# Attention softmax: the negated row maximum as the bias of ScalarE's exponential, VectorE as the copier of the transposed probabilities, other step distances

## The reference

```python
qkv = x @ Wqkv_w.T + Wqkv_b
q = qkv[..., :nf].reshape(nb, ns, 12, 16).transpose(0, 2, 1, 3)
k = q
v = q
w = jnp.einsum('bhqd,bhkd->bhqk', q, k) * (1.0 / jnp.sqrt(16.0))
mask = jnp.tril(jnp.ones((ns, ns)))
w = jax.nn.softmax(w * mask - 1e10 * (1.0 - mask), axis=-1)
a = jnp.einsum('bhqk,bhkd->bhqd', w, v)
return a.transpose(0, 2, 1, 3).reshape(nb, ns, nf) @ Wproj_w.T + Wproj_b
```

## Time and profile before

| | |
|---|---|
| median of three runs | 4598.12 us (4597.52 to 4603.08) |
| the profiled execution's own time | 4601.28 us |
| its span, first to last instruction | 4599.5 us |
| mean granted TensorE clock | 0.949 |
| busy over the span: TensorE, VectorE, ScalarE, GpSimd | 90%, 71%, 52%, 70% |

### The profile page before, as it was taken

How to read it: one execution, slowest core, us unless ns; L and a number is a source line. 1 busy time by engine, 2 the same in 40 slices (tenths; PEclk the granted TensorE clock), 3 DMA queues, 4 the chain that set the end, 5 groups by cost and what they waited for, 6 DMA issues and landing times. The chain is left out here.

```text
span 4599.5 us, 63372 instructions
## 1 busy us (share of the span) xinstructions
PE 4145.6 (90%) x17184; PEld 2234.8 (49%) x17184; DVE 3250.3 (71%) x5016; ACT 2413.6 (52%) x4880; POOL 3215.3 (70%) x1671
## 2 busy tenths in 40 slices
PE   7988958996999999999999999999999974999994
PEld 5666646672344344344334434433433434666773
DVE  5777762121899999999899999999989986112124
ACT  3566632223766766666676666667667544222221
POOL 3233213441999999999999999999999971444441
PEclk7999987997999999999999999999999987999997
DMA  1000023451343333433333333333333321344466
GB/s 34 25 21 23 15 64 87 122 151 52 108 119 116 120 112 112 124 112 120 120 115 112 112 115 121 113 115 116 122 112 115 111 85 49 109 117 118 134 185 227
DMA packets 264754, 478.66 MB, mean 104 GB/s; under 512 B 37044, under 2 KB 174084, under 8 KB 264548
## 3 DMA queue, kind: packets, MB, share of 16 engines
q1 hardware_dynamic: 235776, 403.02, 27.8%
q0 software_dynamic: 28032, 73.17, 6.4%
q10 hardware_dynamic: 740, 0.49, 0.0%
HBM read 409.60 MB, written 41.81 MB: 98 GB/s over the span
## 5 line engine op out<-in xcount | busy, mean ns | idle before, releaser
L1818 POOL TENSOR_TENSOR m_xh<-m_u,m_Bb 128x1536 f32<-128x1536 f32 x512 | 1776.9, 3539 | 58.1 <-DVE m_u L1689 44.9
L1745 PE MATMUL bank<-m_xh,ident 128*128 128x512 f32 x3072 | 1459.7, 611 | 36.3 <-POOL m_xh L1807 36.3
L1787 DVE TENSOR_TENSOR_SCAN bank<-bank,m_xh 128x512 f32<-128x512 f32 x864 | 1039.0, 1216 | 45.1 <-ACT bank L1774 41.9
L1774 ACT ACTIVATE bank<-m_dt,m_Ac 128x508 f32<-128x508 f32 x1536 | 1024.7, 683 | 38.4 <-DVE m_xh L1787 38.4
L1745 PEld LDWEIGHTS bank<-m_xh,ident 128*128 128x128 f32 x3072 | 577.2, 194 | 828.6 <-issue 737.1
L1787 DVE TENSOR_TENSOR_SCAN m_xh<-bank,m_xh 128x512 f32<-128x512 f32 x672 | 787.7, 1207 | 71.5 <-ACT bank L1774 66.0
L1807 POOL TENSOR_TENSOR m_xh<-m_xh,m_Cb 128x1536 f32<-128x1536 f32 x224 | 791.2, 3532 | 4.8 <-DVE m_xh L1787 4.5
L1798 DVE TENSOR_TENSOR m_xh<-bank,m_Cb 128x512 f32<-128x512 f32 x864 | 580.8, 672 | 9.8 <-DMA m_Cb<-BC_rows 9.8
L1204 ACT ACTIVATE f1t_h<-bank,f1t_b 128x512 f32<-128x512 f32 (+1 forms) x276 | 142.8, 589 | 471.3 <-PE bank L1239 471.3
L1593 PE MATMUL bank<-m_xp,m_dg 128*128 128x512 f32 x768 | 352.4, 601 | 3.7 <-DVE m_u L1689 1.4
L1134 POOL DMA_INDIRECT rows_y<-f1t_y,f1t_home x142 | 140.3, 988 | 272.7 <-DVE f1t_y L1175 243.4
(11 more groups left out here) (367 smaller groups left out, 6002.0 us busy)
## 6 DMA issues: line engine op xcount, KB each, us to landing
m_Bb<-BC_rows SPq DMA_DIRECT2D x256, 512.0 KB, 4.9
m_Cb<-BC_rows SPq DMA_DIRECT2D x256, 512.0 KB, 4.1
f1t_w<-f_w SPq DMA_DIRECT2D x46, 576.0 KB
m_r<-m_dt POOLq DMA_DIRECT2D x32, 768.0 KB, 7.4
f1t_w1a<-f_w SPq DMA_DIRECT2D x46, 384.0 KB
f0t_w<-f_w SPq DMA_DIRECT2D x22, 576.0 KB
f1c_yg<-rows_y SPq DMA_DIRECT2D x16, 768.0 KB, 8.3
f1t_w1b<-f_w SPq DMA_DIRECT2D x92, 96.0 KB
```

The lines of the kernel that those rows point to most:

```text
L1745: mm = pe.matmul(bank[:, c, :], K.ident[:, :], xh[n % NX][:, c, :], start=False, stop=(d == 1 and n == NS - 1))
L1774: act.activation(o[:, :, lo:hi], seqs(dt[d][:, c, :])[:, :, lo:hi], ACT.Exp, scale=Ac[:, c, n:n + 1]).then_inc(s_dA, 1)
L1787: dve.tensor_tensor_scan(o, bank[:, RING[d][p], way], xh[n % NX][:, c, way], 0.0, ALU.mult, ALU.add).then_inc(s_h, 1)
L1818: pool.tensor_tensor(xh[n % NX][:, :, :], u[d][:, :, :], Bb[q % RB][:, n % QN, :].unsqueeze(1).to_broadcast([P, DC, TOK]), ALU.mult).then_ ...
```

## The change

VectorE takes the maximum with its sign turned (`negate=True`) and no longer subtracts. ScalarE takes the exponential straight from the score bank, head by head, since the bias is one value a row: three instructions of 128 columns in place of one of 384, each adding one to `s_exp`. The scale 1/4 moves into Q: the copies into qT multiply by 16^(-1/4), which the product of Q with itself squares; the mask's constant shrinks by the same factor 4. The copy of the transposed probabilities moves from ScalarE (`act_pT`) to VectorE (`dve_pT`, right behind `dve_unit`). A score bank is now free when the three exponentials are done. Q's last block is waited for only before the last of the three heads. All distances are new.

```diff
@@ -180,7 +180,7 @@
         s_xn, s_gam, s_h1, s_h1kept = sem("xn_ready"), sem("gamma_done"), sem("h1_ready"), sem("h1_kept")
         s_z, s_zTps, s_zT = sem("z_ready"), sem("zTps_ready"), sem("zT_ready")
         s_qps, s_q = sem("qps_ready"), sem("q_ready")
-        s_sc, s_mx, s_sub, s_exp = sem("scores_ready"), sem("max_ready"), sem("sub_ready"), sem("exp_ready")
+        s_sc, s_mx, s_exp = sem("scores_ready"), sem("max_ready"), sem("exp_ready")
         s_pT, s_pTc, s_pv = sem("probsT_ready"), sem("probsT_copied"), sem("pv_ready")
         s_OT, s_O, s_V = sem("heads_copied"), sem("heads_back"), sem("V_cleared")
         s_ri, s_at, s_aT, s_aTc = sem("rowsum_inv"), sem("att_ready"), sem("attT_ready"), sem("attT_copied")
@@ -188,11 +188,11 @@
 
         OB, TB, FB = (5, 6), 4, 7
         UN = G * RG
-        LE, LT, LU, LV = 3, 4, 5, 9
-        LC, LO, LN, LA, LB, LR, LH = 9, 10, 12, 14, 14, 15, 15
-        PE_AT = {"emb0": 2, "emb1": 3, "zT0": 10, "zT1": 11, "q0": 11, "q1": 12, "q2": 13, "q3": 14, "q4": 15}
+        LE, LT, LU, LV = 0, 2, 2, 7
+        LC, LO, LN, LA, LB, LR, LH = 7, 8, 9, 10, 11, 13, 14
+        PE_AT = {"emb0": 2, "emb1": 3, "zT0": 9, "zT1": 10, "q0": 11, "q1": 12, "q2": 13, "q3": 14, "q4": 15}
         DVE_AT = {"onehots": 0, "emb0": 2, "emb1": 3, "stats1": 3, "norm1": 4, "stats2": 7, "norm2": 8}
-        ACT_AT = {"keep": 10, "zT0": 10, "zT1": 11, "q0": 12, "q1": 12, "q2": 13, "q3": 14, "q4": 15}
+        ACT_AT = {"keep": 8, "zT0": 9, "zT1": 10, "q0": 11, "q1": 12, "q2": 13, "q3": 14, "q4": 15}
 
         WEIGHTS = (
             (gam[:, :], A["ln_gamma"].partition_broadcast(P)), (bet[:, :], A["ln_beta"].partition_broadcast(P)),
@@ -219,7 +219,7 @@
                 pool.iota(col_i[:, :], pattern=[[0, 2]], base=0, channel_multiplier=1).then_inc(cleared, 1)
                 pool.wait_ge(cleared, 2)
                 pool.affine_select(out=mask[:, :, :], in_=mask[:, :, :], compare_op=ALU.is_ge,
-                                   fill=-4.0 * BIG, base=0, pattern=[[0, HC], [-1, P]], channel_multiplier=1).then_inc(cleared, 1)
+                                   fill=-BIG, base=0, pattern=[[0, HC], [-1, P]], channel_multiplier=1).then_inc(cleared, 1)
                 pool.wait_ge(cleared, 3)
                 pool.iota(col_i[64:128, 1:2], pattern=[[0, 1]], base=0, channel_multiplier=1).then_inc(cleared, 1)
                 pool.wait_ge(cleared, 4)
@@ -360,12 +360,13 @@
                 dve.wait_ge(s_sc, n + 1)
                 s_ps = bank[:, u % RG, 0:HC * P].rearrange("p (c k) -> p c k", c=HC)
                 if u >= NE or not isinstance(g, int) or g > 0:
-                    dve.wait_ge(s_pT, n - NE + 1)
-                dve.reduce_max(mx[:, u % NE, :], s_ps, AX).then_inc(s_mx, 1)
-                dve.wait_ge(s_mx, n + 1)
-                dve.tensor_tensor(S[:, u % NE, :, :], s_ps,
-                                  mx[:, u % NE, :].unsqueeze(2).to_broadcast([P, HC, P]),
-                                  ALU.subtract).then_inc(s_sub, 1)
+                    dve.wait_ge(s_exp, (n - NE + 1) * HC)
+                dve.reduce_max(mx[:, u % NE, :], s_ps, AX, negate=True).then_inc(s_mx, 1)
+
+            def dve_pT(dve, g, u):
+                n = g * UN + u
+                dve.wait_ge(s_pT, n + 1)
+                dve.tensor_copy(ST[:, u % NE, :, :], bank[:, TB, 0:HC * P].rearrange("p (c k) -> p c k", c=HC)).then_inc(s_pTc, 1)
 
             def dve_norm_att(dve, g, j):
 
@@ -393,6 +394,7 @@
                 for u in units:
                     if u < UN:
                         dve_unit(dve, g, u)
+                    unit(dve_pT, dve, g, u, LU)
                     for step, lag in ((dve_residual, LH), (dve_norm_att, LN)):
                         tile(step, dve, g, u, lag)
                     for name, step in front.items():
@@ -427,7 +429,7 @@
 
                 act.wait_ge(s_qps, g * 5 + k + 1)
                 if k >= 2:
-                    act.copy(qT[i][:, k - 2, :], bank[:, front(g, f"q{k}"), :]).then_inc(s_q, 1)
+                    act.activation(qT[i][:, k - 2, :], bank[:, front(g, f"q{k}"), :], ACT.Copy, scale=HD ** -0.25).then_inc(s_q, 1)
                 else:
                     b = k
                     if isinstance(g, int) and g == 0:
@@ -436,13 +438,13 @@
                              bank[:, front(g, f"q{k}"), 0:2 * C].rearrange("p (j h d) -> p j h d", j=2, h=HEADS)).then_inc(s_q, 1)
 
             def act_exp(act, g, u):
-                act.wait_ge(s_sub, g * UN + u + 1)
-                act.activation(S[:, u % NE, :, :], S[:, u % NE, :, :], ACT.Exp, scale=HD ** -0.5).then_inc(s_exp, 1)
-
-            def act_pT(act, g, u):
                 n = g * UN + u
-                act.wait_ge(s_pT, n + 1)
-                act.copy(ST[:, u % NE, :, :], bank[:, TB, 0:HC * P].rearrange("p (c k) -> p c k", c=HC)).then_inc(s_pTc, 1)
+                s_ps = bank[:, u % RG, 0:HC * P].rearrange("p (c k) -> p c k", c=HC)
+                act.wait_ge(s_mx, n + 1)
+                if u >= NE or not isinstance(g, int) or g > 0:
+                    act.wait_ge(s_pT, n - NE + 1)
+                for c in range(HC):
+                    act.activation(S[:, u % NE, c, :], s_ps[:, c, :], ACT.Exp, bias=mx[:, u % NE, c:c + 1]).then_inc(s_exp, 1)
 
             def act_OT(act, g, j):
                 n = g * G + j
@@ -460,7 +462,6 @@
             def act_body(act, g, nxt, i, units):
                 for u in units:
                     unit(act_exp, act, g, u, LE)
-                    unit(act_pT, act, g, u, LU)
                     tile(act_OT, act, g, u, LC)
                     tile(act_aT, act, g, u, LB)
                     if u < UN:
@@ -531,15 +532,15 @@
             def pe_scores(pe, g, j, i):
 
                 n = (g * G + j) * RG
-                if j == 0 and isinstance(g, int) and g == 0:
-                    pe.wait_ge(s_q, HC + 2)
-                elif j == 0:
-                    pe.wait_ge(s_q, g * 5 + HC + 2)
+                if j == 0:
+                    pe.wait_ge(s_q, g * 5 + (5 if isinstance(g, int) and g == 0 else 4))
                 for r in range(RG):
                     if j >= 1 or not isinstance(g, int) or g > 0:
-                        pe.wait_ge(s_sub, n - RG + r + 1)
+                        pe.wait_ge(s_exp, (n - RG + r + 1) * HC)
                     pe.matmul(bank[:, r, 0:HC * P], K.identb[:, :], mask[:, :, :], start=True, stop=False)
                 for c in range(HC):
+                    if j == 0 and c == HC - 1:
+                        pe.wait_ge(s_q, g * 5 + 5)
                     for r in range(RG):
                         q = qT[i][32 * r:32 * r + HD, c, j * P:(j + 1) * P]
                         mm = pe.matmul(bank[:, r, c * P:(c + 1) * P], q, q, start=False, stop=(c == HC - 1))
@@ -548,7 +549,7 @@
 
             def pe_probsT(pe, g, u):
                 n = g * UN + u
-                pe.wait_ge(s_exp, n + 1)
+                pe.wait_ge(s_exp, (n + 1) * HC)
                 if u >= 1 or not isinstance(g, int) or g > 0:
                     pe.wait_ge(s_pTc, n)
                 for c in range(HC):
```

## The result

The changed kernel took 4818.51 us in the median of four runs (4786.12 to 4830.02) beside 4597.82 us for the kernel before on the same chip: 1.0467 times as long, 95% interval [1.0411, 1.0523], 221 us more. The prediction said 4738 us, [4640, 4850], slower at 0.86: side and range hold, the point is 80 us short. The profiled span is 4806.7 us against 4599.5, 207 more.

What follows compares the result with a forecast made beforehand. No engine is full; engines wait for each other in a ring. Fifteen groups at +9.0 us (135) plus three bare intervals at 1.67 (5) give +140 us on the 4598.1 median: 4738 us, range 4640 to 4850.

Steps and rivals of the forecast that it cites:

- The new wait: Attention phase: work queued behind VectorE's copy waits for TensorE's same-step transposes, delaying TensorE; 13.9 us a group against 4.9.
- residual waits: TensorE's probabilities times V waits for VectorE's residual, queued behind the copy; 1.02 us a sequence.
- the attention rows: TensorE's attention-row transposes wait for VectorE's normalisation; 1.30 us a sequence, plus 0.57 (one-hots) and 2.2 (first LayerNorm) a group.
- z: Second LayerNorm's output, preparing the next group: ready 3.3 us after the scores, TensorE ready at 1.5; +1.8 us a group.
- TensorE's clock: Attention phase, outside the sum: if a quarter ran at the lower clock, +80 us, giving 4820.
- The argument against it: Against the clock at the lower level for most of the phase: 35 us at 1.00 with 4 us of idleness.
- the period: Time of one group of four sequences, one-hots to one-hots; every 43 to 45 us, from 35.12 before.
- the bare intervals of the last group: Sequences in the last group, which prepares no next one; 7.81 us each in place of 6.14.
- The operations: Attention phase: VectorE's copy 0.56 us for a subtraction of 0.557; ScalarE's exponentials 0.37 each, 0.9 for three, covered.
- The faster case: Rival: transposes done before VectorE reaches the copy, saving 1.9 us a group, 31 us in all; 4567 us; chance 0.10.
- The cheaper chain: Rival: preparation steps find cover, only the 2.32 us of waiting a sequence remains; 4669 us; chance 0.12.
- The slow clock: Rival: TensorE's clock at the lower level for most of the attention phase; 340 us more at worst, half 4900; chance 0.06.

Runs made afterwards that it cites:

- x3: Changed kernel with VectorE's copy of the transposed probabilities moved last in VectorE's step; 4634.6 us, ratio 1.0085.
- x4: Changed kernel with VectorE's copy of the transposed probabilities one step later (LU = 3 in place of 2); 4658.0 us, ratio 1.0128.
- x2: Kernel before, with its own operations but the step distances and tables of the change; 4729.5 us, ratio 1.0286.
- y3: Kernel before with only the bias exponential from PSUM, at distance 0; old distances, ScalarE's copy of transposed probabilities first in its step; 4706.0 us, ratio 1.0235.
- z1: y3 with the exponential moved behind everything else in ScalarE's step; 4666.8 us, ratio 1.0157.
- y1: Changed kernel with TensorE's two longest waits for the attention row filled by 24 unread mask products a group; 4775.7 us, ratio 1.0383.
- y2: Changed kernel's operations with the distances of before (exponential at 0) and VectorE's copy ahead of the maximum; 4756.2 us, ratio 1.0344.

## Why the prediction was right, and where it was short

**The new wait** was right in place and nearly in size. Each group was to wait 13.9 us, 9.0 more than before. The group from 390.91 waits 47.73 - 34.88 = 12.85 us, and by the same reading (busy time by window) the kernel before waits 3.95 in the 35 us of the earlier trace rows: 8.9 more. (The forecast had TensorE's own work at 30.2 us a group, where it is busy 31.05, so its 13.9 and its 4.9 are both about 1 us too large, and the difference hides that.) Over the phase it is 132.5 us where the sum had 140. By its parts, a sequence's residual waits 59.2 / 64 = 0.93 us (1.02 forecast); the attention rows wait 100.4 / 16 = 6.3 a group (4 x 1.30 + 0.57 + 2.2 = 8.0 forecast). In the group from 390.91 the row behind the one-hots waits 1.78 (1.87 forecast), two others 1.28 and 1.18 (1.30), and the one behind the first LayerNorm 2.66 (3.5), so the LayerNorm was priced too high. z waits 20.5 us in the phase, 1.4 a group (1.8). x3 and x4 show the mechanism by taking it away.

**TensorE's clock** is the term that was mis-sized. The prediction held it out of the sum and gave +80 us beside it, if a quarter of the phase ran at the lower level; it measured 74.5 us, at a mean clock of 0.81 where 0.96 stood before. With that sentence in the sum the forecast would have been 4820. That the two figures agree is in part luck. In the rows the level is 0.50 or 1.00, so the mean clocks put an estimated 8% of the phase before and 38% now at the lower one, 30 points more and not a quarter; and these cost 74.5 / (0.30 x 508.2) = 0.49 of TensorE's work, an estimate too, where 0.7 was taken.

The argument against it was that 4 us of idleness in 35 left the clock at 1.00. But those were short waits, none over 0.9 us from 300 to 440 us; the new ones last up to 2.7 us and add up to 12.85 us a group. Length alone doesn't decide: the kernel before fell to 0.50 at 415.9 us behind waits of 0.50 and 0.72 us, one of the five falls that the prediction counted (it left out the phase's start, at 0.50 from 43.8 to 67.8 us), and the last group of the changed kernel fell at 776.7 within a wait of 1.00 us, while the waits of 1.00 to 1.29 us named above did nothing. The Trainium skill says ("TensorE: Matmul & The Clock Gate", HAM oscillation — how this bites in real kernels) of a kernel that waits for DMA between short bursts of matmuls that the clock is throttled again at every one of these waits, and the price paid each time instead of once. The trace agrees that it is paid again and again, twice in the group from 390.91 us, but not behind every wait. The two groups shown have mean clocks of 0.70 and 0.86.

For the same reason the period came out at 47.7 us in the later groups, up to 54 in the earlier ones, for 43 to 45, and the bare intervals of the last group at 9.38, 8.95 and 11.30 us (scores at 770.94, 780.32, 789.27 and 800.57) for 7.8, with the clock at 0.5 in part of each.

**The operations** were priced right. Copy: 0.556 us (0.56). Exponential: 0.365 (0.37), three in 0.88 (0.9). Maximum and copy start 0.46 to 0.47 apart, as taken. The exponentials don't hold the masks, as read above. Idle time before the copy: 294 us, forecast over 150. L364's own fell from 103.3 to 60.0, as said.

**The rivals.** The faster case asked that the transposes be done before VectorE comes to the copy; x4 all but fulfils that (L369 idle 24.3 us) and is still 1.28% slower than before, with the transposes waiting for exponentials and copy. So the prediction's +31 us of gain on VectorE's units was not there to be had at these distances. The cheaper chain had 4.4 us more a group; it was 8.9. The slow clock came in part, as estimated above. The reason given for the slowdown was also too narrow: it named VectorE's copy, and x2 and y3, in which VectorE copies nothing, lose 133 and 111 us. What the three have in common is an operation that waits for another engine's work of the same step; that it is the whole of x2's and z1's loss wasn't shown. What the exponential from PSUM can reach with a better order stays open.

## What to carry to other kernels

Where engines keep a written order, read a step distance as slack: an operation whose input is made in the same step locks what stands behind it, so give it a step, or put it where only late work follows, and then look for the lock's next place. Count a bank's release as well: an operation that frees an input early, as the subtraction did, lets the next engine run several steps behind. Where the waits of TensorE grow from tenths to microseconds, put its clock into the sum, from rows at the lower level, and not beside it.

## What was unexpected of the hardware

The cost of the clock differs between groups with the same work and about the same waiting: in the changed kernel 41.80 us busy and 10.25 idle at a clock of 0.70 in the group from 189.08, 34.88 and 12.85 at 0.86 in the one from 390.91. The four runs spread over 44 us (0.9%), with mean clocks from 0.922 to 0.937, where the kernel before spread over 8 to 19 us in its batches of four and seven. The cost isn't a fixed share of the waiting either: in the table, y1 left aside, the extra busy time is 0.14 to 0.91 of the extra idle time, and x2 and y2, with 104 and 105 us more idle, pay 29 and 62 us at mean clocks of 0.92 and 0.84. And the fall is not tied to the wait itself: at 393.4 TensorE is at work again and the level drops only at 394.4, while at 408.1 it drops within the wait.
